# Row sums of the second attention layer: ones as the stationary operand, or the weights

## The reference

```python
q = jnp.einsum('bte,ef->btf', emb, Wq) + bq
k = jnp.einsum('bml,le->bme', latent, Wk) + bk
v = jnp.einsum('bml,le->bme', latent, Wv) + bv
w = jnp.einsum('bte,bme->btm', q, k) * scale
w = jax.nn.softmax(w, axis=1)                 # over the queries t
pred = jnp.einsum('btm,bme->bte', w, v)
x = pred + emb                                # then a layer norm with gamma and beta
```

## Time and profile before

| | before |
|---|---|
| three timed runs | 1164.41, 1165.70, 1165.85 us |
| the profiled execution, its own time | 1164.51 us |
| span of its records | 1162.6 us |
| TensorE busy, share of the span | 98% |
| VectorE, ScalarE, GpSimd busy | 79%, 77%, 83% |
| granted TensorE clock, mean | 0.997 of full speed |

### The profile page before, as it was taken

How to read it: one execution, slowest core, us unless ns; L and a number is a source line. 1 busy time by engine, 2 the same in 40 slices (tenths; PEclk the granted TensorE clock), 3 DMA queues, 4 the chain that set the end, 5 groups by cost and what they waited for, 6 DMA issues and landing times.

```text
span 1162.6 us, 25505 instructions
## 1 busy us (share of the span) xinstructions
PE 1137.9 (98%) x7917; PEld 1058.8 (91%) x7917; DVE 923.2 (79%) x2148; ACT 893.0 (77%) x1859; POOL 967.3 (83%) x768
## 2 busy tenths in 40 slices
PE   9989999999999999999999999999999999999995
PEld 7789999999999999999999999999999999999984
DVE  4667888878878878878878788887887887887887
ACT  3568788788788788778778878878878778877763
POOL 3458898898888888888889889889888888888865
PEclk9999999999999999999999999999999999999998
DMA  8666676676676676676667667667667667667631
GB/s 314 202 186 204 218 230 210 217 240 209 213 233 214 214 238 210 213 235 213 219 227 227 211 217 230 211 216 231 219 211 237 211 212 238 210 214 236 191 120 68
DMA packets 131697, 249.05 MB, mean 214 GB/s; under 512 B 15696, under 2 KB 88912, under 8 KB 123344
## 3 DMA queue, kind: packets, MB, share of 16 engines
q1 hardware_dynamic: 130656, 247.59, 66.0%
q10 hardware_dynamic: 1008, 1.06, 0.3%
HBM read 165.16 MB, written 83.43 MB: 214 GB/s over the span
## 4 chain that ended last, share of the span: by engine, by line
PE 92%; DMA 2%; DVE 2%; POOL 2%; issue 1%; ACT 1%; SPq 0%; POOLq 0%; DVEq 0%; ACTq 0%
PE bank L382 88%; PE bank L522 1%; PE bank L460 1%; DMA yT_raw<-y_dram 1%; PE bank L548 1%; POOL Y L1515 0%; PE bank L529 0%; DMA y_dram<-y_blk 0%; SPq L270 0%; POOL Y L1518 0%; DMA PT_raw<-E_dram 0%; DVE y_blk L1037 0%; DMA gT<-g_dram 0%; POOLq L69 0%; DVE R L1029 0%
## 5 line engine op out<-in xcount | busy, mean ns | idle before, releaser
L1446 POOL TENSOR_TENSOR xT_lo<-IN,xT_hi 128x1024 fp32r<-128x1024 f32 (+1 forms) x64 | 153.5, 2399 | 25.3 <-ACT xT_hi L671 25.3
L1515 POOL TENSOR_TENSOR Y<-Y,gamma_b 128x512 f32<-128x512 f32 x124 | 157.8, 1294 | 19.6 <-ACT Y L824 19.6
L1518 POOL TENSOR_TENSOR Y<-Y,beta_b 128x512 f32<-128x512 f32 x124 | 157.8, 1295 | 0.0
L1446 POOL TENSOR_TENSOR yT_lo<-yT_raw,yT_hi 128x1024 fp32r<-128x1024 f32 x63 | 151.4, 2404 | 5.1 <-ACT yT_hi L671 5.0
L382 PE MATMUL bank<-yT_hi,A_hi 128*128 128x256 f32 x512 | 144.4, 282 | 2.4 <-issue 2.4
L382 PE MATMUL bank<-xT_hi,A_hi 128*128 128x256 f32 x512 | 144.8, 283 | 1.1 <-DVE A_lo L1218 1.1
L382 PE MATMUL bank<-xT_hi,A_lo 128*128 128x256 f32 x512 | 144.5, 282 | 0.0
L382 PE MATMUL bank<-xT_lo,A_hi 128*128 128x256 f32 x512 | 144.2, 282 | 0.0
L382 PE MATMUL bank<-yT_lo,A_hi 128*128 128x256 f32 x512 | 144.2, 282 | 0.0
L382 PE MATMUL bank<-yT_hi,A_lo 128*128 128x256 f32 x512 | 143.7, 281 | 0.0
L1446 POOL TENSOR_TENSOR cT_lo<-IN,cT_hi 128x512 fp32r<-128x512 f32 x64 | 82.5, 1289 | 62.2 <-ACT cT_hi L671 62.2
(11 more groups left out here) (142 smaller groups left out, 4288.8 us busy)
## 6 DMA issues: line engine op xcount, KB each, us to landing
IN<-in_packed SPq DMA_DIRECT2D x63, 1024.0 KB, 7.3
R<-in_x SPq DMA_DIRECT2D x64, 512.0 KB, 3.5
y_dram<-y_blk SPq DMA_DIRECT2D x252, 128.0 KB, 2.5
yT_raw<-y_dram SPq DMA_DIRECT2D x63, 512.0 KB, 3.6
out<-Y SPq DMA_DIRECT2D x63, 512.0 KB, 3.1
E_dram<-E_blk SPq DMA_DIRECT2D x256, 64.0 KB, 1.9
PT_raw<-E_dram SPq DMA_DIRECT2D x64, 256.0 KB, 2.7
gT<-g_dram SPq DMA_DIRECT2D x64, 128.0 KB, 7.1
```

Source lines behind the costliest of these rows:

```text
L1446: return nc.gpsimd.tensor_tensor(dst, src, fp(hi), ALU.subtract)
L1515: nc.gpsimd.tensor_tensor(y[:, q, :], y[:, q, :], gamma_b[:, :], ALU.mult).then_inc(Y_mul, 1)
L1518: last = nc.gpsimd.tensor_tensor(y[:, q, :], y[:, q, :], beta_b[:, :], ALU.add)
```

## The change

The operands of the row sum change places. The weights become stationary, 128 queries at a time, and the first two columns of the ones move. So the sum of query p comes out on partition p, and no transposing is needed. Two equal columns are made per half q; `scol` shrinks to 4 columns, and one VectorE instruction copies them from PSUM. That instruction also gets a wait on `pred_seed` of the sequence before (the seeds that read `scol`).

```diff
-        scol = sb("scol", [P, ST, 32])
+        scol = sb("scol", [P, 2 * ST])
...
                 pe.wait_ge(w_sums_lo, n.count())
-                for t, part in enumerate(w_sums):
-                    last = nc.tensor.matmul(s_bank[:, 0:S], ones[:, :], part[:, :], start=(t == 0), stop=(t == 1))
+                for q in range(ST):
+                    for t, part in enumerate(w_sums):
+                        last = nc.tensor.matmul(s_bank[:, 2 * q:2 * q + 2], part[:, q * P:(q + 1) * P], ones[:, 0:2],
+                                                start=(q == 0 and t == 0), stop=(t == 1), skip_group_check=True)
...
                 parts = [w[a][:, t, :] for a in range(2) for t in range(ST)]
-                for t, part in enumerate(parts):
-                    last = nc.tensor.matmul(s_bank[:, 0:S], ones[:, :], part, start=(t == 0), stop=(t == 3))
+                for q in range(ST):
+                    for t, part in enumerate(parts):
+                        last = nc.tensor.matmul(s_bank[:, 2 * q:2 * q + 2], part[:, q * P:(q + 1) * P], ones[:, 0:2],
+                                                start=(q == 0 and t == 0), stop=(t == 3), skip_group_check=True)
...
-                    copy(pred_bank[q][:, :], bv1_b[:, :], scale=scol[:, q, 0:1]).then_inc(pred_seed, 1)
+                    copy(pred_bank[q][:, :], bv1_b[:, :], scale=scol[:, 2 * q:2 * q + 1]).then_inc(pred_seed, 1)
...
                 dve.wait_ge(s_full, n.count())
-                for i in range(NB):
-                    group = slice(32 * i, 32 * i + 32)
-                    row = s_bank[group, 0:S].rearrange("p (q i t) -> p q i t", q=ST, i=NB)[:, :, i, :]
-                    last = nc.vector.transpose(scol[group, :, :], row)
-                last.then_inc(s_set, 1)
+                first(dve, pred_seed, n.count(2, 1, back=1))
+                nc.vector.tensor_scalar(scol[:, :], s_bank[:, 0:2 * ST], 1.0, None, ALU.mult).then_inc(s_set, 1)
```

More of the change, by code:

```diff
@@ L1154, in add_s @@
                 dve.wait_ge(s_set, T(3).count())
-                nc.vector.scalar_tensor_tensor(y, bv1_b[:, :], scol[:, q, 0:1], y, ALU.mult, ALU.add
+                nc.vector.scalar_tensor_tensor(y, bv1_b[:, :], scol[:, 2 * q:2 * q + 1], y, ALU.mult, ALU.add
                                                ).then_inc(s_added, 1)
```

## The result

The changed kernel takes 1178.3 us (median of 4 runs, 1176.76 to 1178.97), the kernel before 1165.5 us in the runs beside them (median of 4, 1164.41 to 1165.85). The ratio is 1.0112, with a 95% interval from 1.0096 to 1.0128: slower by 12.8 us. The forecast was 1178.0.

The account below looks back on a forecast made before the run. TensorE's queue was taken to bound the kernel, paid 60 times: 1164.51 + 12.6 for sixty bodies + 0.4 for the last sequences = 1177.5 us, 1178.7 on the median's level; 1178.0 was given, range 1174 to 1182.5.

Parts of the forecast that it names:

- The price of a 2-column matmul: Row sum on TensorE: each 2-column matmul with its 128x128 load costs 0.112 us, within 0.109 to 0.119.
- one-column rows: Set-up's one-column fp32 matmuls, whose weight loads stand 0.110 us apart; the near case in width for the price.
- the transposes: Eight 128-column transposes near the end, loads 0.109 us apart; lower end of the price for a 2-column matmul.
- The sum for a body: TensorE in each body: four matmuls at 0.448 us replace 0.238 us, +0.21 us, between +0.20 and +0.24.
- The rival by columns: Row sum: cost goes by moving columns, loads hide; four cost 0.02 us, kernel falls to 1152 us; chance 0.03.
- The one of an unhidden load: Row sum: load not hidden or made twice, 0.19 us each, +0.52 a body, 1196 us; chance 0.05.
- in-between pitch: Row sum: 2-column fp32r matmuls 0.06 to 0.10 us apart; 0.08 gives 1170 us; chance 0.05.
- The last sequences: Last four sequences, where TensorE does wait: +0.4 us in all, with bounds -0.5 to +0.8.
- VectorE's saving shows in three places: Last sequences: some 0.85 us saved starts seeds of `T(2)` earlier, the same before `add_s`, and once more for `T(1)`.
- the +0.2 for `T(2)`: Last sequences: row sum of `T(2)` delays scores of `T(3)`, which lead to GpSimd's last work: +0.2 us.
- The added wait: VectorE's copy waits on `pred_seed` of the sequence before, met some 15 us in advance: 0.

Follow-up runs that it names:

- copy-only kernel: Kernel before with its two 256-column matmuls, but one four-column VectorE copy replacing four transposes, plus the wait on `pred_seed`; 1165.3 us, 0.9999 of the kernel before.
- Eight in place of four: Changed kernel with each small row-sum matmul of a body issued twice, the copy halving the sum; 1206.5 us, 1.0354 of the kernel before.
- 128-column experiment: Changed kernel with 128 columns of ones moving instead of 2 in the row sum; 1177.0 us, 1.0099 of the kernel before.
- second trace: Changed kernel run once more, unaltered, for another profile of its end part; 1178.2 us, 1.0113 of the kernel before.

## Why the prediction was right, and where it was off

- **What bounds the kernel.** TensorE's queue alone. The copy-only kernel (0.9999 with 58 us less on VectorE) and the one with one matmul less (7.6 us faster) show it from both sides.
- **The price of a 2-column matmul.** 0.112 us was taken from the one-column rows and the transposes. Eight in place of four gave 0.112. The sum for a body was +0.21, measured +0.21. The step that carried the forecast was to price a narrow matmul by what doesn't depend on its columns, and to read that from two near rows. That it is the load that sets it fits every trace, but wasn't parted from the matmul's own share.
- **The rival by columns** (1152) falls with the 128-column experiment and with the rows. The one of an unhidden load (1196) as well: the loads are 0.11 to 0.12 apart though each record is 0.19 long. The in-between pitch didn't occur with fp32r.
- **What I had not priced:** that 0.11 us is the price with 4-byte operands. The rows of before hold no other, so the forecast didn't need it, but the change would have been one for the better with bf16 halves.
- **The last sequences.** +0.4 us was forecast, with -0.5 to +0.8; between the two traces it was about +1.2 without the sixtieth body, outside these bounds. 0.7 of it lies before `Pc_` of the last sequence, in the stretch that varies as much without the change. Behind it is +0.64 (46.91 against 46.27, and 46.91 again in the second trace), inside the bounds but not for the reasons given. Wrong was the step "VectorE's saving shows in three places" with no loss from it: an earlier VectorE cost GpSimd 0.5 us, and GpSimd sets the end. And the +0.2 for `T(2)` didn't come. From its row sum to GpSimd's gamma it is 1144.97 - 1139.21 = 5.76 us before and 1159.10 - 1153.34 = 5.76 after (5.75 in the copy-only kernel).
- **The added wait** held up nothing; no wait for `pred_seed` is in the trace, and the copy-only kernel, which has it too, is as fast as the one before.

The median moved by 12.8 us, and 60 bodies of 0.212 make 12.7 of it. The 1.2 us of the end part and the 0.7 of the set-up are of the two profiled executions; runs of one kernel lie up to 2 us apart and more, so the medians can't tell them. For the same reason it is partly luck that the forecast of 1178.0 came within 0.3 us of the median; what is borne out is the +0.21 us of a body.

## What to carry to other kernels

When TensorE's queue is full, count its matmuls with their loads, not the columns of the narrow ones: here a matmul of 2 to 128 columns with its 128x128 fp32r load cost 0.112 us, nearly as much as a matmul of 256 columns (0.119). Work taken off an engine with slack gave nothing in 60 bodies and cost 0.5 us at the end, where it made two engines meet. If a small product has to have its data stationary, 2-byte halves for it are worth a try: here they turned 12.8 us of loss into 2.2 us of gain.

## What the runs showed of the hardware that was not expected

- Four pairs of a 128x128 bf16 load and a 2-column matmul took about 0.025 us each, four fp32r ones 0.112 each. The first bf16 load behind an fp32r matmul was not started together with that matmul, as loads of the same type are; the block gained 0.25 us and not the 0.35 that 4 x (0.112 - 0.025) make.
- Stationary bf16 ones and moving bf16 sums of 256 columns made no difference in time to fp32r ones (0.9997).
- GpSimd's addition of 128x512 on SBUF took 1.28 us without and 1.74 with VectorE's addition of 128x512 on SBUF beside it, its 128x2 step 0.67 and 1.12. VectorE's addition of 2 columns took up to 1.33 us beside GpSimd's addition. 0.8 us of overlap at its end did not lengthen GpSimd's addition (1.29).
